# A gather of graph edges in which a tile of 128 edges that spans two windows of nodes is fetched once, and TensorE reads its place in the ring from a table

## The reference

```python
x = x + segment_sum(layernorm(x)[src] * edge_weight[:, None], dst) @ W.T + b        # 100000 edges, sorted by dst
x = x + ffn0(layernorm(x))          # router top-k over the nodes, 256 -> 1024 -> 256
msg = (layernorm(x) @ weight[edge_type])[src] * edge_weight1 * sigmoid(gate[edge_type, src])
x = x + relu(segment_sum(msg, dst))
x = x + moe(layernorm(x))           # 8 experts, top 2, 256 -> 1024 -> 256
```

## Time and profile before

| | us |
|---|---|
| median of 3 runs (lowest, highest) | 3868.61 (3863.25, 3874.06) |
| the profiled execution's own time | 3869.11 |
| its span | 3866.7 |
| busy: TensorE, DVE, ACT, POOL | 2527.5, 2377.0, 974.9, 2039.0 |

### The profile page before, as it was taken

The page is one execution under the profiler, slowest core; times in us unless marked ns, Lnnn a source line. Parts: engine busy times, 40 slices in busy tenths (PEclk is TensorE's granted clock), DMA queues, the critical chain, the costliest instruction groups (busy, mean ns, idle before and its releaser), DMA issues. The chain is left out here.

```text
span 3866.7 us, 70366 instructions
## 1 busy us (share of the span) xinstructions
PE 2527.5 (65%) x17373; PEld 1751.7 (45%) x17374; DVE 2377.0 (61%) x7860; ACT 974.9 (25%) x2424; POOL 2039.0 (53%) x2078
## 2 busy tenths in 40 slices
PE   1745556667777449999945445445454328999997
PEld 1433344556666324444423333333333216777775
DVE  7534556676888677777754555666666564545554
ACT  1300011222333326666610000000011133333332
POOL 1477777777776100000057777777777204555554
PEclk9966777888889769999976666666766659999998
DMA  3233333333333114444454555554334272223222
GB/s 121 86 105 104 103 103 102 103 102 102 100 102 88 44 44 195 195 195 195 195 189 145 152 167 149 151 155 116 112 114 115 61 242 43 46 47 46 45 48 35
DMA packets 170324, 440.94 MB, mean 114 GB/s; under 512 B 41488, under 2 KB 95888, under 8 KB 163744
## 3 DMA queue, kind: packets, MB, share of 16 engines
q0 software_dynamic: 101984, 250.24, 24.7%
q1 hardware_dynamic: 60528, 183.32, 12.6%
q10 hardware_dynamic: 7760, 6.83, 0.5%
HBM read 283.78 MB, written 156.47 MB: 114 GB/s over the span
## 5 line engine op out<-in xcount | busy, mean ns | idle before, releaser
L712 POOL DMA_INDIRECT g_msg<-table,idx x1664 | 1623.3, 976 | 507.1 <-issue 385.6
L776 PE MATMUL psum<-g_msg,g_hot 128*128 128x256 f16 x1664 | 613.0, 368 | 969.3 <-issue 832.7
L731 DVE TENSOR_SCALAR g_hot<-iota,g_cols 128x128 f16<-128x128 f16 x3328 | 771.4, 336 | 32.6 <-DVE g_cols L727 30.1
L776 PEld LDWEIGHTS psum<-g_msg,g_hot 128*128 128x128 f16 x1664 | 216.3, 130 | 1092.7 <-issue 1023.8
L777 PE MATMUL psum<-g_msg,g_hot 128*128 128x256 f16 x1664 | 611.1, 367 | 0.0
L778 PE MATMUL psum<-g_msg,g_hot 128*128 128x256 f16 x1664 | 605.3, 364 | 0.0
L1258 DVE SCALAR_TENSOR_TENSOR t_row<-psum,t_gate,t_row 128x256 f16<-128x256 f32 x800 | 350.4, 480 | 152.8 <-ACT t_row L1301 152.8
L1301 ACT ACTIVATE t_row<-psum,t_gate 128x256 f16<-128x256 f32 x800 | 335.2, 470 | 185.8 <-PE psum L1334 185.8
L1651 POOL DMA_INDIRECT out<-ex_y,ex_to x112 | 207.1, 1849 | 247.4 <-DMA out<-ex_y,ex_to 167.7
L795 ACT ACTIVATE side<-psum x98 | 37.6, 383 | 1160.8 <-PE psum L778 1160.8
L708 POOL MEMSET g_zeros<- 128x256 f32 x2 | 0.6, 311 | 618.6 <-POOLq L1217 613.7
(11 more groups left out here) (360 smaller groups left out, 4780.5 us busy)
## 6 DMA issues: line engine op xcount, KB each, us to landing
table<-t_row SPq DMA_DIRECT2D x50, 2048.0 KB, 6.3
g_msg<-table,idx POOLq DMA_INDIRECT x1664
piece_stage<-in_w SPq DMA_DIRECT2D x32, 512.0 KB, 5.3
w_halves<-piece_halves SPq DMA_DIRECT2D x32, 512.0 KB, 3.2
w<-w_halves SPq DMA_DIRECT2D x8, 2048.0 KB, 22.5
rows<-sc_row ACTq DMA_DIRECT2D x52, 128.0 KB
acc<-in_x SPq DMA_DIRECT2D x5, 1280.0 KB, 13.6
table<-t_row SPq DMA_DIRECT2D x25, 256.0 KB, 2.1
```

The source lines that it names most:

```text
L712: pool.indirect_dma_start(out=msg[step % RING][:, :], out_offset=None, in_=table, in_offset=bass.IndirectOffsetOnAxis(ap=t[f"idx{g}"][:, s ...
L731: last = nc.vector.tensor_scalar(hot[b][:, (2 * k + h) * P:(2 * k + h + 1) * P], t["iota16"][:, :], c3[:, k, LOCAL - first:LOCAL - first + ...
L776: pe.matmul(ps, hi, row[:, 0:D], start=False, stop=False, skip_group_check=True)
```

## The change

Each tile is fetched once, in its own order: 784 transfers for 832 steps. The ring is one buffer of 32 places, and tile n lies in place n modulo 32. TensorE therefore no longer knows at which place a step's rows lie. `prepare` adds to `code`, for every batch, the number of tiles that must have come and the eight places (20 numbers instead of 16 for a batch, of which 11 and then 8 are read), and makes a table `freed`, which tells for every batch of 8 tiles its last step. SyncE stands between the engines: `arrive` waits for a batch of 8 transfers and adds 8 to `tiles_in`, for which TensorE waits; `release` reads `freed`, waits until that step is multiplied, and adds 1 to `ring_free`, for which POOL waits once in 8 transfers. The moves of the pieces are put into the same loop of SyncE, one store and one load after the release of tile batches 1, 2, 5, 6, ... 61, 62. `prepare` gathers three fields a step instead of five; the row numbers now come by tile, straight from memory, by two DMAs.

```diff
@@ prepare, DVE
+            chain(nc.vector.tensor_scalar(early_w[:, :], batch_ends[:, :], ends[:, :], None, ALU.is_ge))
...
+            chain(nc.vector.tensor_tensor(start_row[:, :], step_no[0:1, :], win_row[:, :], ALU.subtract))
+            chain(nc.vector.tensor_copy(step_at[:, :], start_row[:, :]))
+            chain(nc.vector.tensor_scalar(code[:, :, MSG_TILES:MSG_TILES + 1], start_row[:, :].rearrange("p (m k) -> p m k", k=BATCH)[0:1, 0:NB, BATCH - 1:BATCH],
+                                          1.0, float(EDGE_ROWS), ALU.add, ALU.min))
+            chain(nc.vector.tensor_scalar(step_at[:, :], step_at[:, :], RING - 1, None, ALU.bitwise_and))
+            chain(nc.vector.tensor_copy(start_row[:, :], step_at[:, :]))
+            chain(nc.vector.tensor_scalar(code[:, :, MSG_AT:MSG_AT + BATCH], start_row[:, :].rearrange("p (m k) -> p m k", k=BATCH)[0:1, 0:NB, :],
+                                          float(2 * D), None, ALU.mult))
...
+            chain(nc.vector.tensor_tensor(t["freed"][:, :], core.bank[7][0:1, 0:TILE_BATCHES], batch_ends[0:1, :], ALU.add))
...
+            dve.wait_ge(types_loaded, 32)
+            chain(nc.vector.scalar_tensor_tensor(out=t["idx1"][:, :], in0=t["idx0"][:, :], scalar=float(RELS), in1=types[:, :],
+                                                 op0=ALU.mult, op1=ALU.add))
...
-                chain(nc.vector.tensor_copy(c[:, k, 0, :], e[:, k, 0, :]))
-
-                chain(nc.vector.scalar_tensor_tensor(out=c[:, k, 1, :], in0=e[:, k, 0, :], scalar=float(RELS),
-                                                     in1=e[:, k, 2, :], op0=ALU.mult, op1=ALU.add))
...
-                nc.vector.tensor_copy(t["idx0"][:, cut], a[:, 0:P])
-                nc.vector.tensor_copy(t["idx1"][:, cut], a[:, P:2 * P])
@@ gather, SyncE
+            def arrive(k, i, b):
+
+                sp.wait_ge(arrived[b], before[b] + 16 * BATCH * (i + 1))
+                sp.sem_inc(tiles_in, BATCH)
+
+            def release(k):
+
+                done = sp.value_load(t["freed"][0:1, bass.ds(k, 1)], min_val=0, max_val=STEPS - 1)
+                sp.wait_ge(mm_done, done + 1 + RING)
+                sp.sem_inc(ring_free, 1)
+
             if pieces:
-                pieces.move(sp)
+                pieces.first(sp)
+            for k in range(AHEAD):
+                arrive(k, 0, k)
+
+            done = 0
+            for kind in range(pieces.kinds if pieces else 0):
+                with sp.Fori(done, done + pieces.count // 2 - 1) as i:
+                    for b in range(BATCHES):
+                        arrive(BATCHES * i + b + AHEAD, i + (b + AHEAD) // BATCHES, (b + AHEAD) % BATCHES)
+                        release(BATCHES * i + b)
+                        if b in (1, 2):
+                            n = 2 * (i - done) + b - 1
+                            pieces.store(sp, kind, n, b - 1)
+                            pieces.load(sp, kind, n + 2, b - 1)
...
@@ gather, POOL
-            for step in range(STEPS):
-
-                pool.wait_ge(mm_done, step + 1)
+            for n in range(EDGE_ROWS):
+                at = n % RING * 2 * D
+                if n >= RING and n % BATCH == 0:
+
+                    pool.wait_ge(ring_free, n // BATCH - BATCHES + 1)
                 pool.indirect_dma_start(
-                    out=msg[step % RING][:, :], out_offset=None, in_=table,
-                    in_offset=bass.IndirectOffsetOnAxis(ap=t[f"idx{g}"][:, step:step + 1], axis=0)).then_inc(arrived[step // BATCH % BATCHES], 16)
+                    out=msg[:, at:at + 2 * D], out_offset=None, in_=table,
+                    in_offset=bass.IndirectOffsetOnAxis(ap=t[f"idx{g}"][:, n:n + 1], axis=0)).then_inc(arrived[n // BATCH % BATCHES], 16)
@@ gather, TensorE
                     pe.wait_ge(hot_done, m + 1 + PAIR)
-                    pe.wait_ge(arrived[b], before + 16 * BATCH * (i + 1))
-                    at = t["code"][0:1, bass.ds(m * CODE, BATCH + BATCH // BANKS)]
+                    at = t["code"][0:1, bass.ds(m * CODE, MSG_TILES + 1)]
...
+                    at = t["code"][0:1, bass.ds(m * CODE + MSG_AT, BATCH)]
...
+                    pe.wait_ge(tiles_in, code[MSG_TILES])
...
-                        row = msg[b * BATCH + k]
-                        pe.matmul(ps, hi, row[:, 0:D], start=False, stop=False, skip_group_check=True)
-                        pe.matmul(ps, hi, row[:, D:2 * D], start=False, stop=False, skip_group_check=True)
-                        pe.matmul(ps, lo, row[:, 0:D], start=False, stop=False, skip_group_check=True).then_inc(mm_done, 1)
+                        row = [msg[:, bass.ds(slot_at[k] + h * D, D)] for h in range(2)]
+                        pe.matmul(ps, hi, row[0], start=False, stop=False, skip_group_check=True)
+                        pe.matmul(ps, hi, row[1], start=False, stop=False, skip_group_check=True)
+                        pe.matmul(ps, lo, row[0], start=False, stop=False, skip_group_check=True).then_inc(mm_done, 1)
```

More of the change, by code:

```diff
@@ L62 @@
 BANKS = 4
-CODE = 16
+CODE = 20
+MSG_TILES = BATCH + BATCH // BANKS
+MSG_AT = MSG_TILES + 1
 NB = STEPS // BATCH
+TILE_BATCHES = EDGE_ROWS // BATCH
 FLUSH = 3
@@ L444, in _ @@
                                     passed[:, k * (STEP_COLS // 2):(k + 1) * (STEP_COLS // 2)], start=True, stop=True)
+            pe.matmul(core.bank[7][0:1, 0:TILE_BATCHES], t["ones"][0:WINDOWS - 1, 0:1], early_w[:, :], start=True, stop=True)
             last_mm = pe.matmul(core.bank[3][0:1, 0:WINDOWS - 1], ends[:, :], t["ident"][0:WINDOWS - 1, 0:WINDOWS - 1],
@@ L615, in __init__, with load, store, first @@
         self.width = [P, D]
-    def move(self, sp):
+    def load(self, sp, kind, n, b):
+        view = self.views[kind]
+        at = view[n:n + 1] if isinstance(n, int) else view[bass.ds(n, 1)]
+        sp.dma_start(self.stage[b][:, :].rearrange("p (c d) -> p c d", c=view.shape[2]), at.rearrange("n p c d -> p (n c) d")).then_inc(self.came[b], 16)
+    def store(self, sp, kind, n, b):
+        sp.wait_ge(self.lo_done, kind * self.count + n + 1)
+        at = self.to[kind][n:n + 1] if isinstance(n, int) else self.to[kind][bass.ds(n, 1)]
+        sp.dma_start(at.rearrange("n p d -> p (n d)"), self.halves[b][:, :]).then_inc(self.left[b], 16)
+    def first(self, sp):
         for b in range(2):
             sp.sem_inc(self.left[b], 16)
[L621 to L639, removed]
-            for b in range(2):
-                store(self.count - 2 + b, b)
+            self.load(sp, 0, b, b)
+    def finish(self, sp):
         for b in range(2):
@@ L665, in gather @@
     rounds = STEPS // RING
-    msg = [w.sb(f"{name}_msg{k}", [P, 2 * D], F16) for k in range(RING)]
-    PAIR = 2
+    msg = w.sb(f"{name}_msg", [P, RING * 2 * D], F16)
+    PAIR, AHEAD = 2, 2
     cols = [w.sb(f"{name}_cols{b}", [P, BATCH * 3], F32) for b in range(PAIR)]
@@ L670, in gather @@
     zeros = w.sb(f"{name}_zeros", [P, D], F32)
-    arrived, before = core.arrived, g * rounds * BATCH * 16
+    arrived, before = core.arrived, [g * 16 * BATCH * (-(-(TILE_BATCHES - b) // BATCHES)) for b in range(BATCHES)]
+    tiles_in, ring_free = core.sems(f"{name}_tiles_in", f"{name}_ring_free")
     cols_done, hot_done, mm_done, bank_free, copied, zeroed = core.sems(*(
```

69 lines of the change are left out of this document (47 added, 22 removed).

## The result

| | before | after |
|---|---|---|
| median of 4 runs (lowest, highest), us | 3869.67 (3863.25, 3874.06) | 3978.05 (3972.69, 3986.24) |
| the profiled execution: own time, span, TensorE's granted clock | 3869.11, 3866.7, 0.814 | 3980.16, 3978.0, 0.807 |
| first gather, first transfer to last matmul | 1075.3 | 1104.1 |
| second gather, the same | 1077.3 | 1161.1 |
| start of the first transfer | 178.0 | 176.5 |

The changed kernel takes **1.0283 times as long, 95% interval 1.0265 to 1.0300: slower by 108 us**. The forecast was 3850, in a range of 3812 to 3888. Of the 111.3 us between the two spans, 28.8 are in the first gather and 83.8 in the second, and prepare gives back 1.6.

What follows compares the result with a forecast made beforehand. POOL's transfers at 1.28 us each were taken as the bound, with DVE and TensorE equally slow at each gather's end. 3869.1 - 27 (first gather) + 10 (second gather) - 2 (prepare) = 3850 us, range 3812 to 3888.

Steps and rivals of the forecast that it cites:

- POOL as the clock, and the change of regime: Both gathers: transfers at 1.28 us each set the pace, until DVE with TensorE is as slow at each gather's end.
- prepare: Setup before the gathers: 7.4 us of DVE work removed, 5.4 added, 2 us saved.
- on a straight line one of eight takes 0.91: TensorE's added table read: eight values cost 0.91 us, on a line through reads of ten values (1.08) and one (0.31).
- A batch starts 1.2 us later: TensorE's batch start after its hot matrices: the second table read, an eleventh value and gaps add 1.2 us, bounds 0 and 1.5.
- The slower rival: Second gather: a batch with a window grows 1.8 us and loads land later, giving 3880 to 3910 us; chance 0.16.
- the closed chain: Second gather: hot matrices, table reads, 24 matmuls, gate product, bias, next hot matrices; 1.2 us paid at every batch with a window.
- In this gather I count half: First gather: DVE goes on without TensorE's answer, so only 0.6 us a batch is charged, 1 us lost in the last stretch.
- the prediction's own lines: First gather by stretch: 19 us saved to 778, 15 to 978, 1 lost to 1254; sum 33, taken as 27 saved.
- The second gather's dense end: Last stretch, 2663 to 3041, 28 of 37 batches with a window at 12.7 us: 391 against 378, 13 us lost.
- the 8 us that DVE was to win back: Second gather, up to 2663: DVE recovers some 8 us of what waits for pieces lost.
- The pieces: Second gather: piece loads cap the gain at 6 us, and late rounds make DVE wait, 11 us lost.
- The table reads hide: Rival: TensorE's sequencer runs ahead, so reads are free where hot matrices are early; 3812 to 3835 us, chance 0.17.

Runs made afterwards that it cites:

- aligned: The changed kernel with the eight places starting at word 12 of a batch's 20 instead of word 11: 3843.88 us, 0.9936 of the kernel before.
- reads_first: The changed kernel with both table reads moved in front of the wait for the hot matrices: 3815.80 us, 0.9867 of the kernel before.
- before_even_read: The kernel before plus a second read of eight values from word 0, values used: 4514.43 us, 0.9956 of the kernel before on the same slow chip.

## Why the prediction was wrong

**POOL as the clock, and the change of regime: right.** Transfers are still 1.28 us each, and TensorE with DVE behind it takes over where windows are dense. So is **prepare**: 1.6 us saved for 2 forecast.

**The failed step: "on a straight line one of eight takes 0.91"**, in the costing of the second table read. The line went through reads of ten values and of one. Both start at a word divisible by four. The new read starts at word 11 of a batch's 20, and costs 1.94. The reads of `code` in all runs fit this list, within 0.06 us: a read that starts at a word divisible by four takes 0.30 us for each whole four words and 0.24 for each word left over; one that starts at an odd word takes 0.24 for every word.

| words, start | us measured | by the list |
|---|---|---|
| 8, word 0 or 12 | 0.60, 0.60 | 2 x 0.30 |
| 10, word 0 | 1.08 | 2 x 0.30 + 2 x 0.24 = 1.08 |
| 11, word 0 | 1.32 | 2 x 0.30 + 3 x 0.24 = 1.32 |
| 12, word 0 | 0.85 | 3 x 0.30 = 0.90 |
| 8, word 1 or 11 | 1.94, 1.94 | 8 x 0.24 = 1.92 |

A read of one value doesn't fit so well: it takes 0.31 on TensorE, not 0.24. What the hardware does to make it so was not tried, nor any start other than those in the table. The trace of the kernel before already held a row against the straight line, which the prediction didn't use: DVE reads three values of the table `slot` from word 1 of four, where the line gives 0.48 us and the list 0.72 (one value takes DVE 0.31 as well).

```profile
L687 DVEq TENSOR_LOAD <-slot x104: 751/756/1128, 338.0 to 3070.7; - x104
```

The Trainium skill, Runtime: NRT & Kernel Launch, section Instruction fetch mechanics, has about 200 ns a register even in bulk. The Trainium skill, Runtime: NRT & Kernel Launch, section Terms, says of these loads that they fetch registers from HBM, and the table here lies in SBUF, so the figure is for another case. The prediction weighed it and turned it down by the row of ten values. The odd read comes near it, 243 ns each; the aligned eight, at 75 ns each, do not.

**"A batch starts 1.2 us later": it was 2.35.** That is the term that was mis-sized: 1.94 + 0.24 for the eleventh value + 0.17 for gaps. The slower rival named the mechanism (the closed chain, "the eight values dearer") and its point of decision, 13.3 us for a batch with a window; the median was 14.06. It had 0.16, and priced the growth at 1.8 us, for 3880 to 3910. The measured 3978 lies beyond it too: no rival reached that far.

**"In this gather I count half": wrong too.** With 2.35 us in full for each batch with a window, the prediction's own lines give for the first gather: 19 us saved up to 778; then 7.6 x 3.9 + 12 x 13.45 = 191 us of work in a stretch of 200, 9 saved; then 5 x 3.9 + 22 x 13.45 = 315 against 276, 39 lost. Sum 11 lost; measured 28.8 lost, forecast 27 saved. With half of it the same lines give 19 + 15 - 14, or 20 us saved. The last stretch comes out: from batch 76, at 966 us, to the end 36 us were lost, and over batches 78 to 102 the mean batch with a window grew by 1.85 us, most of the 2.35. The stretches before it don't: by batch 76 the change had saved 7 us where these lines give 28. The aligned version had saved 23 by then, so part of that is the dear read again; how it is lost there was not followed. The loop is closed in this gather as well: DVE's wait for the window's transposed rows goes through TensorE.

```profile
DVE f_xlo L982 <- ACT f_xhi L1019: 113.9, 27, 8.7
```

in the first gather after, and before

```profile
DVE f_xlo L922 <- ACT f_xhi L959: 72.3, 21, 9.5
```

That transposition stands behind the batch's 24 matmuls, so it comes as late as they do. This is read from the rows; no run undid it alone.

**The second gather's dense end.** Its line becomes 9 x 3.9 + 28 x 13.85 = 423 against 378, 45 lost instead of 13. Measured from batch 62 to the end: 61 us lost, with the 8 us that DVE was to win back among what did not come.

**The pieces: the mechanism right, the size off.** DVE was to wait in batches 56 to 61 and the gain up to there to be capped at 6 us. Counted from the start of the gather, the first matmul of batch 50 came 3.2 us sooner than before, that of batch 62 23.2 us later: between them 26 us lost, forecast 11. The waits began at batch 4, in 26 of 32 pieces. Part of the loss is again the dear read: aligned alone has batch 62 20.4 us sooner.

**With a read near the price assumed, the time comes out, in part by luck.** The aligned version has the eight values at 0.60 where 0.91 was assumed, its matmuls start 1.0 us later than before where 1.2 was assumed, and it takes 3843.88 for the forecast's 3850. Its gathers come out at 19.4 and 2.4 us saved, where 27 saved and 10 lost were forecast: both off by 8 to 12 us, and against each other, so the sum is better than its terms.

**"The table reads hide" (0.17)** did not come true of the code as written, since the reads stand behind the wait; it is what reads_first makes of it. The Trainium skill, TensorE: Matmul & The Clock Gate, section Architectural detail, with its queue of 64 instructions, was cited there; it speaks of weight loads, and no row could show a table read that runs ahead of the array. The trace of reads_first does: in its second gather the first read begins before the earlier matmuls have ended in 102 of 103 batches, and the gap of 0.25 us says that both reads can be done before the last hot matrix.

## What to carry to other kernels

Price a table read by where it starts and how many words it has, not by a line through other lengths: pad the table so that each read starts at a multiple of four words and is a multiple of four long (a pad of one word was worth 134 us here). Put reads that depend on nothing ahead of a wait, since TensorE's sequencer did these reads while it would have stood still, and look for loops in which the waited-for engine waits back. Slack makes such costs look small: an open microsecond in each batch was worth 5 to 27 us while 832 transfers set the pace, and with 784 it was worth 99 at first and 25 when most of it was gone, so measure a saving with the next bound already moved.

## What was not expected of the hardware

- Eight values in 1.94 us or 0.60, by the word at which they start; twelve in 0.85, eleven in 1.32.
- Waiting once in eight transfers instead of at each leaves the 0.30 us between two transfers as it was.
- One of the chips ran the kernel before in 4533 us where the others took 3868 to 3873. There, in the first gather of before_even_read, TensorE goes through the feed-forward matmuls in pairs:

```profile
1003.15 0.22 PE L976 MATMUL psum<-f_xhi,w_hi 128*128 128x128 f16 x1 [1.19 <-issue]
1003.21 0.22 PE L977 MATMUL psum<-f_xlo,w_hi 128*128 128x128 f16 x1
1004.58 0.26 PE L978 MATMUL psum<-f_xhi,w_lo 128*128 128x128 f16 x1 [1.15 <-issue]
1004.64 0.31 PE L976 MATMUL psum<-f_xhi,w_hi 128*128 128x128 f16 x1
1006.01 0.27 PE L977 MATMUL psum<-f_xlo,w_hi 128*128 128x128 f16 x1 [1.06 <-issue]
```

with over 1 us before each pair in which it waits for nothing that the profile shows. In the kernel before, elsewhere, the same matmuls follow at 0.05 to 0.11 us:

```profile
1003.17 0.31 PE L973 MATMUL psum<-f_xhi,w_hi 128*128 128x128 f16 x1
...
1003.28 0.31 PE L974 MATMUL psum<-f_xlo,w_hi 128*128 128x128 f16 x1
```

The gather took 1465 us instead of 1080 there, and POOL waited for TensorE. The granted clock of the gather was 0.72 against 0.80, but the quickest 24 matmuls take 2.51 us on both chips. It looks as if TensorE's instructions came late; no run tests that, and it stays open.
